# A time-warping wave run from both corners at once instead of forward over the whole table

## The reference

```
D = sqrt(max(aa + bb - 2 a @ b.T, 0))            # 77 keys by 512 tokens, for each batch
R[i, j] = D[i, j] + min(R[i-1, j], R[i, j-1], R[i-1, j-1])
i, j = 76, 511                                   # walk back along the cheapest path
while not at (0, 0):
    expanded[j] += a[i]
    (i, j) = the predecessor with the least R (diagonal, then up, then left)
x = x + tanh(g) * expanded
```

## Time and profile before

| what | value |
|---|---|
| time, median of 3 runs | 796.64 us (796.64, 796.64, 797.85) |
| span of the profiled execution, first to last instruction | 794.8 us |
| what lies around the span, against the median run | 1.8 us |
| DVE busy, share of the span | 77% |
| PE busy, share of the span | 83% |

### The profile page before, as it was taken

One profiled execution on the slowest core, in us unless ns is written; L12 is line 12 of the kernel. 1 busy time (PEld: TensorE's weight loads), 2 busy tenths in 40 slices (PEclk: granted clock), 3 DMA queues, 4 the chain that ended last, 5 costly groups with the idle time before them and its releaser, 6 DMA issues.

```text
span 794.8 us, 13507 instructions
## 1 busy us (share of the span) xinstructions
PE 658.4 (83%) x3446; PEld 499.5 (63%) x3446; DVE 610.5 (77%) x2037; ACT 397.0 (50%) x702; POOL 395.5 (50%) x399
## 2 busy tenths in 40 slices
PE   5653330188999999999999969998799999999995
PEld 2321110176787787877878846665678787877884
DVE  5799999687777777777777785688877777777774
ACT  5533110044565565555565644545456565565653
POOL 4047870036566666665666653000155666656663
PEclk9655555559999999999999975999799999999999
DMA  5424442205877677786776600000146765666761
GB/s 145 78 66 133 137 124 44 47 1 122 153 162 147 139 160 140 147 156 135 158 153 129 134 1 1 2 2 12 37 84 136 161 153 131 159 149 136 160 134 53
DMA packets 73810, 85.90 MB, mean 108 GB/s; under 512 B 39097, under 2 KB 51754, under 8 KB 70760
## 3 DMA queue, kind: packets, MB, share of 16 engines
q1 hardware_dynamic: 66714, 75.05, 44.7%
q0 software_dynamic: 4320, 9.68, 4.1%
q10 hardware_dynamic: 2734, 0.69, 0.4%
HBM read 76.69 MB, written 8.70 MB: 107 GB/s over the span
## 4 chain that ended last, share of the span: by engine, by line
PE 67%; DVE 23%; issue 5%; ACT 2%; DMA 2%; POOL 1%; DVEq 0%; SPq 0%; POOLq 0%; ACTq 0%
PE bank L1034 7%; PE bank L1035 7%; PE bank L1036 7%; PE bank_quad L1190 7%; PE bank_pair L1036 7%; PE bank_pair L1034 7%; PE bank_pair L1035 7%; PE bank_quad L1187 6%; PE bank_quad L1188 6%; DVE arena L1491 3%; PE bank_pair L1083 2%; DVE arena L1487 2%; PE bank L1126 2%; DVE arena L1445 2%; DVE arena L1435 2%
## 5 line engine op out<-in xcount | busy, mean ns | idle before, releaser
L695 POOL TENSOR_TENSOR act_lo<-arena,act_hi 128x512 fp32r<-128x512 f32 x232 | 300.5, 1295 | 193.6 <-ACT act_hi L868 190.8
L1724 DVE TENSOR_TENSOR bank_pair<-arena,bank_pair 128x512 f32<-128x512 f32 x220 | 152.5, 693 | 103.9 <-ACT arena L882 72.9
L882 ACT ACTIVATE arena<-bank 128x512 f32<-128x512 f32 x232 | 139.0, 599 | 185.6 <-PE bank L1036 185.6
L1732 DVE TENSOR_TENSOR arena<-bank_pair,arena 128x512 f32<-128x512 f32 x220 | 152.1, 691 | 16.7 <-DMA arena<-scr_mask 4.5
L868 ACT ACTIVATE act_hi<-arena 128x512 fp32r<-128x512 f32 x232 | 144.6, 623 | 12.8 <-DVE arena L1722 7.1
L1034 PE MATMUL bank_pair<-xn_hi,w_hi 128*128 128x512 f32 x232 | 92.6, 399 | 2.9 <-DVE arena L1722 2.1
L1190 PE MATMUL bank_quad<-act_lo,w_hi 128*128 128x512 f32 x232 | 92.5, 399 | 3.0 <-POOL act_lo L695 3.0
L1034 PE MATMUL bank<-xn_hi,w_hi 128*128 128x512 f32 x232 | 93.8, 404 | 0.1
L1035 PE MATMUL bank<-xn_hi,w_lo 128*128 128x512 f32 x232 | 92.6, 399 | 0.0
L1036 PE MATMUL bank<-xn_lo,w_hi 128*128 128x512 f32 x232 | 92.5, 399 | 0.0
L1036 PE MATMUL bank_pair<-xn_lo,w_hi 128*128 128x512 f32 x232 | 92.3, 398 | 0.0
(11 more groups left out here) (220 smaller groups left out, 1072.6 us busy)
## 6 DMA issues: line engine op xcount, KB each, us to landing
arena<-scr_mask SPq DMA_DIRECT2D x94, 512.0 KB, 6.7
scr_w<-prep_out POOLq DMA_DIRECT2D x25, 192.0 KB, 2.2
w_raw<-scr_w SPq DMA_DIRECT2D x25, 192.0 KB, 6.3
w_raw<-in_L_ffn_expert_gate_k SPq DMA_DIRECT2D x32, 64.0 KB, 5.9
w_raw<-in_L_ffn_expert_up_k SPq DMA_DIRECT2D x32, 64.0 KB, 5.7
w_raw<-in_L_ffn_expert_down_k SPq DMA_DIRECT2D x64, 32.0 KB, 5.2
prep_in<-in_L_ffn_wg POOLq DMA_DIRECT2D x21, 64.0 KB, 2.3
prep_in<-in_L_ffn_wu POOLq DMA_DIRECT2D x21, 64.0 KB, 2.1
```

Source lines behind the costliest of these rows:

```text
L695: nc.gpsimd.tensor_tensor(act_lo[:, k % 2, :], act_a[:, k % 2, :], act_hi[:, k % 2, :].bitcast(F32), ALU.subtract).then_inc(FF[f]["alo"], 1)
L882: nc.scalar.activation(act_s[:, k % 2, :], ps[4 + k % 2][:], ACT.Silu).then_inc(FF[f]["silu"], 1)
L1724: nc.vector.tensor_tensor(ps[6 + i][:], act_s[:, i, :], ps[6 + i][:], ALU.mult).then_inc(FF[f]["t"], 1)
L1732: nc.vector.tensor_tensor(act_a[:, i, :], ps[6 + i][:], mask[:, j, 512 * k:512 * (k + 1)], ALU.mult).then_inc(FF[f]["act"], 1)
```

## The change

The table is cut between keys 38 and 39. Lanes at partitions 0 to 63 warp forward from the first corner over keys 0 to 38, lanes at partitions 64 to 127 warp the reversed table from the last corner over the other keys, in the same instructions. There are now 15 lanes of 35 columns for each batch and direction, and 39 + 14 = 53 slots a wave. From slot 38 on the two comparisons carry a per-lane factor (`scalar_tensor_tensor` with a column of `lane_table`). While the last 15 slots run, TensorE adds the two halves' costs column by column (`meet`); then DVE finds the best column (`meeting`) and TensorE spreads it over the lanes; both halves walk back from there, in 53 slots.

With it come: each half's own distance matmuls, on 64 and 39 columns of the array, the second with its tokens reversed; a reversed half of the context, which passes through a scratch in DRAM on ScalarE's queue; constants for the lanes on GpSimd; lane loads of all 53 slots before slot 0; path cells written in two halves; path parts stored once for each half and loaded in four DMAs (d = 0 on SP, d = 1 on ScalarE). The loads of the weight preparation move from GpSimd's to SP's queue, the value projections between the first 12 groups. TensorE does `meet` right after group 9.

```diff
-    CH = 16
-    CW = S // CH
-    SLOTS = KEYS + CH - 1
+    CH, CW = 15, 35
+    COLS = CH * CW
+    PAD = COLS - S
+    HALF = (KEYS + 1) // 2
+    DROWS = [slice(0, HALF), slice(64, 64 + HALF)]
+    KROWS = 64 + HALF
+    SLOTS = HALF + CH - 1
+    MEET = HALF - 1
+    FIRST_SLOT = [0, 64]
+    LSLOT = 64 + SLOTS
...
+    MEET_AT, VALUE_AT = 9, 14
...
-        ON_PARTS = [(44, SLOTS), (12, 44), (0, 12)]
+        PIECES = [(SLOTS - PIECE * (g + 1), SLOTS - PIECE * g) for g in range(SLOTS // PIECE - 1)]
+        PIECES.append((0, PIECES[-1][0]))
+        ON_PARTS = [(25, SLOTS), (5, 25), (0, 5)]
+        ON_PIECES = [1 + [p[0] for p in PIECES].index(first) for first, last in ON_PARTS]
...
+                    sp.wait_ge(s_cz, 2)
...
+        def store_dist(engine, d, b):
+            first = DROWS[d].start
+            engine.dma_start(at(scr_d[b], first * CW, [[CW, HALF], [LANE + CW, CH], [1, CW]]),
+                             d2[DROWS[d], b, :].rearrange("i (c w) -> i c w", w=CW)).then_inc(s_dst[b], 16)
+        def load_lanes(engine, d, b):
+            engine.wait_ge(s_dst[b], 32)
+            first = FIRST_SLOT[d]
+            engine.dma_start(dl[lanes(d, b)].rearrange("c s w -> c (s w)"),
+                             scr_d[b, :, first:first + SLOTS].rearrange("c s w -> c (s w)")).then_inc(s_dld, 16)
+        def lanes_laid(engine):
+            engine.wait_ge(s_dld, 16 * 2 * B)
+        def store_path(engine, part, d):
+            first, last = ON_PARTS[part]
+            engine.wait_ge(s_on, 2 * ON_PIECES[part])
+            engine.dma_start(scr_on[d, :, :, first:last, :].rearrange("b c s w -> (b c) (s w)"),
+                             on[64 * d:64 * (d + 1), first:last].rearrange("c s w -> c (s w)")).then_inc(s_onst[d], 16)
+        def load_path(engine, part, d):
+            first, last = ON_PARTS[part][0], (HALF, LOWER)[d] if part == 0 else ON_PARTS[part][1]
+            engine.wait_ge(s_onst[d], 16 * (part + 1))
             for b in range(B):
+                cells = pmask[64 * d + first:64 * d + last, b, PAD * (1 - d):PAD * (1 - d) + COLS].rearrange("i (c w) -> i c w", w=CW)
+                engine.dma_start(cells if d == 0 else cells[:, ::-1, :],
+                                 at(scr_on[d, b], first * CW,
+                                    [[CW, last - first], [ON_LANE + CW, CH], [1, CW]])).then_inc(s_path[d], 16)
+        def load_prep(engine, g, r0, r1):
+            j = g % 2
+            if g >= 2:
+                engine.wait_ge(s_pt, g - 1)
+            if r1 - r0 < P:
+                engine.wait_ge(s_pzero, 1)
...
+            for g in range(2):
+                load_prep(sp, g, *prep_span(g))
             sp.wait_ge(s_blank, 1)
-            sp.dma_start(scr_d.rearrange("b c s w -> (b c) (s w)"),
-                         dl[0:B * CH].rearrange("p s w -> p (s w)")).then_inc(s_zero, 16)
-            sp.wait_ge(s_zero, 16)
+            for first in range(0, LSLOT, SLOTS):
+                n = min(SLOTS, LSLOT - first)
+                sp.dma_start(scr_d[:, :, first:first + n].rearrange("b c s w -> (b c) (s w)"),
+                             dl[0:B * CH, 0:n].rearrange("p s w -> p (s w)")).then_inc(s_zero, 16)
+            sp.wait_ge(s_zero, 16 * -(-LSLOT // SLOTS))
             for b in range(B):
                 sp.wait_ge(s_dist, b + 1)
-                store_dist(sp, 0, b)
-                store_dist(sp, 1, b)
-                if b >= 1:
-                    load_lanes(sp, 0, b - 1)
-            load_lanes(sp, 0, B - 1)
-            for b in range(B):
-                load_lanes(sp, 1, b)
-            lanes_laid(sp, 0)
+                for d in range(2):
+                    store_dist(sp, d, b)
+                if b in (1, 2):
+                    for d in range(2):
+                        load_lanes(sp, d, b - 1)
+            for b in (2, 3):
+                load_lanes(sp, 0, b)
+            for g in range(2, GROUPS[1]):
+                load_prep(sp, g, *prep_span(g))
             for part in range(len(ON_PARTS)):
-                for b in range(B // 2):
-                    store_path(sp, part, b)
-                for b in range(B // 2):
-                    load_path(sp, part, b)
+                store_path(sp, part, 0)
+                load_path(sp, part, 0)
             sp.wait_ge(FF[0]["wlo"], 1)
             raw0(2, 0)
...
+                nc.gpsimd.memset(ctx_sb[p0:p0 + 32], 0.0).then_inc(s_cz, 1)
...
+            def lane_tables():
+                act.wait_ge(s_lt, 1)
+                nc.scalar.activation(lane_table[:], ps[7][:, 0:TABLE], ACT.Copy).then_inc(s_lc, 1)
+                nc.scalar.activation(rst[:, 0, 0:1], ps[7][:, CORNER:CORNER + 1], ACT.Copy).then_inc(s_lane, 1)
...
+            act.dma_start(scr_ctx, at(ctx_1024, (KEYS - 1) * H, [[KEYS * H, B], [-H, LOWER], [1, H]])).then_inc(s_crev, 16)
...
-                    value_block(*CHUNK_HEADS[g - 6])
+                if VALUE_AT <= g < VALUE_AT + len(CHUNK_HEADS):
+                    value_block(*CHUNK_HEADS[g - VALUE_AT])
             act.wait_ge(s_rt, 1)
...
-                pe.wait_ge(s_ctn, 1)
+                pe.wait_ge(s_ctn, 1 if b == 0 else 3)
                 pe.wait_ge(s_xhi, b + 1)
-                nc.tensor.matmul(dist_bank(b), ctxT_neg[:, b, :], xT0[:, b, :], start=True, stop=False)
+                if b == B - 1:
+                    pe.wait_ge(s_lane, 1)
+                top, bottom = dist_bank(b)[0:64, :], dist_bank(b)[DROWS[1], :]
+                nc.tensor.matmul(top, ctxT_neg[:, b, 0:64], xT0[:, b, :], start=True, stop=False)
+                nc.tensor.matmul(bottom, ctxT_neg[:, b, DROWS[1]], xT0[:, b, ::-1], start=True, stop=False)
                 pe.wait_ge(s_sq, b + 1)
-                nc.tensor.matmul(dist_bank(b), ones[:, 0:KEYS], sq[:, b % 2, :], start=False, stop=True).then_inc(s_ab, 1)
+                nc.tensor.matmul(top, ones[:, 0:64], sq[:, b % 2, :], start=False, stop=True)
+                nc.tensor.matmul(bottom, ones[:, 0:HALF], sq[:, b % 2, ::-1], start=False, stop=True).then_inc(s_ab, 1)
...
+            def project_values(c, b):
+                pe.wait_ge(s_c4, 1)
+                pe.wait_ge(s_sq, B)
                 rows = CHUNK_ROWS[c]
+                out_b = ps[1 + c][0:rows, P * b:P * (b + 1)]
+                keys = ctxT4[:, b].rearrange("p i k -> p (i k)")[:, P * c:P * c + rows]
+                nc.tensor.matmul(out_b, keys, w4[:, 2, :], start=True, stop=False)
+                nc.tensor.matmul(out_b, ones[0:1, 0:rows], bv_row[:], start=False, stop=True).then_inc(s_vp, 1)
+            def meet(c):
+                pe.wait_ge(s_scan, MEET + c + 1)
+                n, first = columns(c), CW * c
+                sums = ps[0][0:B, :]
+                nc.tensor.matmul(sums[:, first:first + n], meet_pick[:, 0, c, :], rst[:, MEET + c + 1, 1:1 + n],
+                                 start=c == 0, stop=False, skip_group_check=True)
+                nc.tensor.matmul(sums[:, S - first - n:S - first], meet_pick[:, 1, c, :], mst[:, (MEET + c) % MST, 0:n][:, ::-1],
+                                 start=False, stop=c == CH - 1, skip_group_check=True).then_inc(s_meet, 1)
...
                 mm.then_inc(s_pt, 1)
+                if g < RCH * B:
+                    project_values(g // B, g % B)
+                if g == MEET_AT:
+                    for c in range(CH):
+                        meet(c)
+                    pe.wait_ge(s_mcol, 1)
+                    nc.tensor.matmul(ps[0][:, 0:1], meet_batch[:], meet_col[:], start=True, stop=True).then_inc(s_mrep, 1)
...
+            def valid(kind, s):
+                return lane_table[:, kind + s - MEET:kind + s - MEET + 1]
             def left_steps(s):
-                nc.vector.tensor_tensor(lg[:, s, 0, :], rst[:, s + 1, 0:CW], mst[:, s % MST, :], ALU.is_lt).then_inc(s_steps, 1)
+                left, least = rst[:, s + 1, 0:CW], mst[:, s % MST, :]
+                if s < MEET:
+                    nc.vector.tensor_tensor(lg[:, s, 0, :], left, least, ALU.is_lt).then_inc(s_steps, 1)
+                else:
+                    nc.vector.scalar_tensor_tensor(lg[:, s, 0, :], left, valid(LEFT_VALID, s), least, ALU.mult,
+                                                   ALU.is_lt).then_inc(s_steps, 1)
...
-                if s in (0, LSPLIT):
-                    lanes_laid(dve, 0 if s == 0 else 1)
+                if s == 0:
+                    lanes_laid(dve)
                 if s >= MST:
                     dve.wait_ge(s_steps, s - MST + 1)
                 nc.vector.stream_shuffle(cur[:, 0:1], prev[:, CW:CW + 1], shift)
                 nc.vector.tensor_tensor(mst[:, s % MST, :], prev[:, 1:CW + 1], prev[:, 0:CW], ALU.min).then_inc(s_upper, 1)
-                nc.vector.tensor_tensor(lg[:, s, 1, :], prev[:, 0:CW], prev[:, 1:CW + 1], ALU.is_le)
+                if s <= MEET:
+                    nc.vector.tensor_tensor(lg[:, s, 1, :], prev[:, 0:CW], prev[:, 1:CW + 1], ALU.is_le)
+                else:
```

(33 more changed lines are left out.)

255 lines of the change are left out of this document (139 added, 116 removed).

## The result

| | before | after |
|---|---|---|
| median of 4 runs | 797.05 us (796.64 to 797.85) | 776.37 us (773.87 to 780.49) |
| profiled execution / its span | see above | 776.3 / 774.6 us |
| slot 0 starts | 34.53 | 46.98 |
| last scan, first backward shuffle | 92.02, 93.18 | 80.69, 84.06 |
| TensorE's product after the path | 156.78 | 138.46 |

The ratio is 0.9747 (0.9718 to 0.9777): 2.5% faster. The forecast was 759.5 with a range of 754 to 769; the time lies above it. Of 37.1 us 20.7 came. The runs of the changed kernel lie 6.6 us apart, those of the one before 1.2.

What follows compares the result with a forecast made beforehand. It took DVE's 118 us of short instructions in a row as the bound. TensorE's product after the path moves from 156.78 to 119.7 (-37.1 us), so the span falls from 794.8 to 757.7; plus 1.8 gives 759.5, range 754 to 769.

Steps and rivals of the forecast that it cites:

- The start: Before slot 0: clears +0.6, distance matmuls +0.3, lane loads +0.9 us, so slot 0 moves from 34.5 to 36.3.
- The context: Reversed half through DRAM on ScalarE's queue: TensorE turns it about 3 us later, adding nothing before slot 0.
- Rival 2: Late start: the reversed context arrives after its slack, slot 0 3 us later, time 762.5; chance 0.06.
- Distance pairs: Distance matmuls before slot 0, doubled in number, share the array in pairs; +0.3 us.
- Rival 3: Distance matmul pairs before slot 0 don't share the array: +3.4 us, time 762.9; chance 0.07.
- Forward wave: DVE's 52 slots of 0.644 us plus 0.3 and 0.4: last scan starts 34.2 behind slot 0.
- Meeting: Between last forward scan and backward wave: products, index search, thresholds and gaps, 3.6 us together.
- Backward wave: DVE's 53 backward slots of 0.709 us each, 37.6 us.
- Preparation: TensorE's weight groups 10 to 24 after the meeting: seven rounds of 4.2 us plus extras, from 74.4 to 105.3.
- Rival 1: Weight preparation keeps its old pace of 2.90 us a group: product at 129.4, time 769.2; wholly or partly 0.18.
- Path parts: Three path parts on ScalarE's queue after the preparation, 13.5 us in all, so product not before 119.7.
- Rival 5: Slower than before: preparation rounds of load and turning above 9.7 us instead of 4.2, reaching 797 and more; chance 0.02.

Runs made afterwards that it cites:

- x3: Changed kernel with SP issuing all eight distance stores as they come ready and the eight lane loads after them, four on ScalarE's queue; 776.35 us.
- c1: x6 with lane loads split: slots 0 to 26 before slot 0, slots 27 to 52 behind all, waited for at slot 27; 771.71 us.
- x6: Changed kernel with 128 slots of scratch per lane instead of 117, pieces still 140 bytes; 769.41 us.
- f1: Changed kernel with 40-column pieces, 124-slot lanes, context in 32 and 6 rows, read-side reversal, meeting behind group 12, path parts cut at slot 9; 762.99 us.
- p1: Changed kernel with TensorE preparing groups 10 to 12 before it waits for the meeting; 775.44 us, ratio 0.9724.
- p2: Changed kernel with the second half's path chunks loaded without reversing them, the reversal left out of the computation; 776.33 us, ratio 0.9744.
- p3: Changed kernel with the second half's chunks reversed on the side that is read, the destination written forwards; 776.33 us.

## Why the prediction was wrong

- **The start is the step that failed.** "I take 2.9 of the span 2.0 to 4.0: +0.9" priced only the loads, and left the store at the 1.79 of the earlier trace rows. The loads were nearly right (3.27). The store on the chain took 7.33, 5.5 more; and SP, still waiting for the landing of batch 1's store (6.74), sent it out 3.0 us after the distances were ready, a wait that the sum doesn't have. With the 1.3 of the next point these are 9.8 of the 10.7 us by which slot 0 came late. The prediction counted bytes and instructions; the new store has almost the same of both, but its pieces of 140 bytes lie at other addresses. What limits it is the store itself, not the queue (x3) or the loads between (c1). The range had no case for it: its bounds were taken for the loads' size, none for the store's form, though it was an operation that the trace of before doesn't show. Other addresses (x6, and f1 with its better start as a whole) give 4.6 and 6.1 of the 10.7 back.
- **The context "about 3 us later: nothing"** was 5.1 late (TensorE turns it at 9.66; it did at 4.60 before), and the last distances 2.2, where 0.9 was counted. Rival 2 named this mechanism; of its 3 us 1.3 came.
- **Distance pairs: right.** The batch of eight instructions at the high clock, in order of time:

```profile
19.39 0.64 PE L1089 MATMUL bank<-arena,ctxT_neg 128*64 128x512 f32 x1
19.40 1.05 PE L1090 MATMUL bank<-arena,ctxT_neg 128*39 128x512 f32 x2
...
20.72 0.59 PE L1093 MATMUL bank<-arena,ones 128*39 128x512 f32 x1
20.73 0.59 PE L1092 MATMUL bank<-arena,ones 128*64 128x512 f32 x1
21.26 0.66 PE L1071 MATMUL bank_quad<-ident,xn 128*128 128x128 f32 x4
```

  The two of a pair start 0.01 us apart, and eight start and end within 1.9 us; one after another they would be 3.4 and more at the 0.43 that the pairs lie apart. Rival 3 falls. So does, here, the sentence of the Trainium skill that the prediction took up ("TensorE: Matmul & The Clock Gate", Part 3, The mechanism), that a weight load overlaps a running matmul only if its row group differs: the loads for the next pairs start at 19.86 and 20.29, under running matmuls on the same 128 rows. The same section of the Trainium skill also names a background weight buffer, into which a load may go ahead; no row here tells whether this is what happens.
- **Forward wave: right.** Last scan 33.7 behind slot 0, for 34.2. **Meeting: right**, 3.4 for 3.6.
- **Backward wave: too short by 7%.** From the first scan (84.35) to the last are 39.34 us for 52 slots, 0.757 each for 0.709, and the last cells end 78.0 behind slot 0 for 75.4. No experiment took this apart; it cost nothing here, since ScalarE's queue ended later still, but in p1 and f1, where that queue waits for the cells, it stands in the chain.
- **Preparation: 34.0 us from group 10 to 24 for 30.9.** Four of the seven rounds took 4.3 to 4.5 for the 4.2 of the sum, with the "two issues 0.8" as forecast, the third counting in the landing. Group 16, with a fourth load that landed in 3.92, took 6.3, group 18 4.9 and group 24 5.4. Group 24's loads went out at 115.02, 1.9 us behind the turning of group 22, where the other rounds of the chain lost less than 0.1: its buffer has to be zeroed first, which GpSimd did at 114.51, behind its store of group 22. That GpSimd's queue "has only stores left and waits for nobody new" overlooked this zeroing, for which SP now waits; before, GpSimd's own queue had both in order. The extra 3.1 are partly made up around them (group 10 0.6 earlier behind slot 0 than forecast, ScalarE 0.65 quicker behind group 24); the preparation's part of the miss is 1.9. Rival 1 (2.90 a group) was too dear, 2.43 was measured.
- **Path parts: 19.7 for 13.5.** "four loads are issued at 0.39 each" took SP's price from the earlier trace rows for ScalarE's reversed loads, which cost 0.73 to 0.90: 4.3 us over eleven issues, and p2 and p3 bring the issues down to 0.38. The rest is landings of 2.3 to 3.2 instead of 1.5 to 2.6.
- **Sign: right; size: 20.7 us for 37.1.** Rival 5 (slower) needed rounds above 9.7 us. Behind the product everything moved along, but for the 1.9 us named above.

Sum: 10.7 of the start, 1.9 of the preparation, 6.2 of the parts are the 18.8 by which the product is late. The median lies 16.9 above the forecast, since those 1.9 us count the other way. f1, with the start and the path parts mended, comes to 762.99, inside the range of 754 to 769; that is no merit of the forecast, which was made for the kernel without these edits.

## What to carry to other kernels

A transfer whose pieces change in size, pitch or distance is a new operation, even if its bytes stay the same: give it a range of its own, and put the wait that stands on its landing into the sum. Take the price of an issue from the same queue and the same form; where a half must be reversed, reverse the side that is read. When loads move to another queue, look for what the old queue's order had settled without a wait, as the zeroing of the last buffer here. When a layout leaves the distance between rows free, try two or three values before anything else: one number moved slot 0 from 47 to 50 down to 42 to 44.

## What the hardware showed that was not expected

- Stores of 1,170 pieces of 140 bytes landed in 5.8 to 8.5 us with 16,380 or 16,384 bytes from lane to lane (x3, whose stores follow one another without a wait, apart), in 3.7 to 7.2 with 17,920. In four kernels with the same start slot 0 lies up to 3.4 us apart.
- The difference lies behind the last packet: 3.6 us from there to the landing of batch 0 in the kernel after, 1.5 in x6.
- 12 bytes of displacement cost pieces of 128 bytes 5 us over four batches (1.0073 in time).
- With all stores issued without a wait the last took 11.24 us to land (x3), and landed no sooner.
- An issue whose destination runs backwards took 0.75 us, the same load with the source running backwards 0.38, with ScalarE's queue for both.
- Open: which property of 16,380 bytes (16,520 in the store) counts, what a row off a multiple of 64 bytes costs by itself, and why the context's load takes 5 us.
